# A three-block transformer layer on one core: attention's small work spread over other engines, and the last head's output tiles on two pairs of banks

## The reference

```python
x = x + 0.5 * ffn(layernorm(x), q_w, k_w, v_w, o_w, sel_v_w, sel_o_w, route_scale)
x = x + attention(layernorm(x), W_qkv, b_qkv, W_out, b_out)
x = x + 0.5 * ffn(layernorm(x), ...)                      # the same weights again
# x: (4, 512, 128) float32
# attention: 16 heads of 8 columns: softmax(q k^T / sqrt(8)) v, then W_out
# ffn: 8 heads of 128 columns, softmax attention in which value and output projection are
#      sums over 8 experts, gated by a top-2 of sigmoid(x @ sel) (normalised, times route_scale):
#   v   = sum_e gate_v[e] * (x @ v_w[h, e])
#   out = sum_h sum_e gate_o[h, e] * (softmax(q k^T / sqrt(128)) v) @ o_w[h, e]
```

## Time and profile before

| | us |
|---|---|
| median of 3 runs (1535.32 to 1540.82) | 1536.66 |
| the profiled execution | 1539.83 |
| its span, first to last instruction | 1538.0 |
| busy in the span: PE / DVE / ACT / POOL | 1477.0 / 1290.4 / 1205.5 / 978.5 |
| attention alone, from the last FFN slot to the first of the second FFN | about 690 to 881 |

### The profile page before, as it was taken

The page is one execution under the profiler, slowest core; times in us unless marked ns, Lnnn a source line. Parts: engine busy times, 40 slices in busy tenths (PEclk is TensorE's granted clock), DMA queues, the critical chain, the costliest instruction groups (busy, mean ns, idle before and its releaser), DMA issues.

```text
span 1538.0 us, 25896 instructions
## 1 busy us (share of the span) xinstructions
PE 1477.0 (96%) x7263; PEld 1104.9 (72%) x7263; DVE 1290.4 (84%) x3434; ACT 1205.5 (78%) x3587; POOL 978.5 (64%) x1719
## 2 busy tenths in 40 slices
PE   7899999999999999988998899999999999999997
PEld 5677888888888888743333358887888788888885
DVE  6899889888988877788878948988898889888885
ACT  3788888888888888748876778888888888888884
POOL 4578877776777677653240135777677767776665
PEclk9999999999999999999988999999999999999999
DMA  6244533322343225302211013333233333333321
GB/s 200 69 137 151 192 137 111 110 110 92 108 145 111 101 105 206 123 15 83 83 55 56 15 55 118 111 112 112 106 111 110 110 117 110 110 110 117 110 83 35
DMA packets 50837, 163.48 MB, mean 106 GB/s; under 512 B 3460, under 2 KB 26630, under 8 KB 34310
## 3 DMA queue, kind: packets, MB, share of 16 engines
q1 hardware_dynamic: 50694, 161.82, 30.0%
HBM read 136.64 MB, written 25.17 MB: 105 GB/s over the span
## 4 chain that ended last, share of the span: by engine, by line
PE 46%; DVE 7%; ACT 2%; issue 2%; POOL 1%; POOLq 0%; DVEq 0%; ACTq 0%
PE bank L523 10%; PE bank L524 10%; PE bank L525 10%; DVE mmax L1457 4%; PE bank L690 3%; PE bank L833 3%; PE bank L798 2%; PE bank L705 2%; PE bank L703 2%; PE bank L704 2%; DVE ot L1351 1%; ACT ot L1041 1%; PE bank L818 1%; PE bank L843 0%; ACT pm L1110 0%
## 5 line engine op out<-in xcount | busy, mean ns | idle before, releaser
L1002 ACT ACTIVATE vt<-bank,gate 128x128 f32<-128x128 f32 x1024 | 293.1, 374 | 105.2 <-PE bank L525 90.9
L1351 DVE SCALAR_TENSOR_TENSOR ot<-bank,gn,ot 128x128 f32<-128x128 f32 x1024 | 288.0, 344 | 70.0 <-ACT ot L1041 50.8
L1626 POOL TENSOR_TENSOR vt<-vt 128x256 f32<-128x256 f32 x256 | 197.8, 773 | 228.7 <-DVE vt L1337 227.9
L1041 ACT ACTIVATE ot<-bank,gn 128x128 f32<-128x128 f32 x1024 | 291.8, 372 | 24.9 <-PE bank L525 19.4
L1337 DVE SCALAR_TENSOR_TENSOR vt<-bank,gate,vt 128x128 f32<-128x128 f32 x1024 | 286.1, 342 | 11.5 <-ACT vt L1002 9.4
L1651 POOL TENSOR_TENSOR ot<-ot 128x256 f32<-128x256 f32 x256 | 197.5, 772 | 90.8 <-DVE ot L1351 86.9
L1360 DVE TENSOR_TENSOR pt<-bank,pt 128x512 fp32r<-128x512 f32 x256 | 175.6, 686 | 69.8 <-ACT pt L1029 69.4
L523 PE MATMUL bank<-wv,xhl 128*128 128x512 f32 x512 | 224.2, 438 | 3.0 <-DVE vt L1337 1.9
L523 PE MATMUL bank<-wo,chl 128*128 128x512 f32 x512 | 206.4, 403 | 7.9 <-DVE chl L1320 5.4
L1018 ACT ACTIVATE pp<-bank,nmin 128x512 f32<-128x512 f32 x256 | 178.1, 696 | 42.2 <-DVE nmin L1327 40.2
L1327 DVE TENSOR_REDUCE nmin<-bank 128x1 f32<-128x512 f32 x256 | 173.8, 679 | 37.0 <-PE bank L525 33.4
(11 more groups left out here) (192 smaller groups left out, 3000.7 us busy)
## 6 DMA issues: line engine op xcount, KB each, us to landing
wv<-wv_split SPq DMA_DIRECT2D x56, 1024.0 KB, 4.8
wo<-wo_split SPq DMA_DIRECT2D x56, 1024.0 KB, 4.8
wv_split<-wv SPq DMA_DIRECT2D x8, 1024.0 KB, 5.0
wo_split<-wo SPq DMA_DIRECT2D x8, 1024.0 KB, 7.1
qk<-qk_rows SPq DMA_DIRECT2D x32, 256.0 KB, 2.9
qk_rows<-qs SPq DMA_DIRECT2D x24, 256.0 KB, 2.9
rawv<-in_L_ffn_v_w SPq DMA_DIRECT2D x8, 512.0 KB, 6.2
rawo<-in_L_ffn_o_w SPq DMA_DIRECT2D x8, 512.0 KB, 8.2
```

The lines of the kernel that those rows point to most:

```text
L1002: last = activation(vt[:, u % 2, e * P:(e + 1) * P], gb[0][:, e * P:(e + 1) * P], ACT.Copy, scale=gate[:, n % 2, k, h * E + e:h * E + e + 1])
L1041: last = activation(ot[:, u % 2, e * D:(e + 1) * D], gb[2][:, e * D:(e + 1) * D], ACT.Copy, scale=gn[:, j % 2, k, e:e + 1])
L1351: last = v.scalar_tensor_tensor(o, gb[3][:, e * D:(e + 1) * D], gn[:, j % 2, k, G + e:G + e + 1], o, ALU.mult, ALU.add)
L1626: own.link(g_.tensor_tensor(a[:, 0:2 * P], a[:, 0:2 * P], a[:, 2 * P:4 * P], ALU.add))
```

## The change

1. **Last head** (its four tiles, in f = 1): the odd tiles' output products go to banks 0 and 1, which the value products have left, instead of 2 and 3, and PE waits for the reading of tile i - 2 rather than i - 1. DVE makes the first fold of 256 columns itself, right after its four instructions and before it releases the tile; POOL makes the two others.
2. **split_maxima** goes from DVE to POOL, in the same step.
3. **over_sums**: ACT copies the group's transposed outputs with their sums out of bank 5 to a new buffer oR (copy_sums, one instruction of 144 columns a group, in the step in which DVE did its part), and this releases the bank. Once a batch, at r = 37 (SUMS), DVE takes one reciprocal of 64 columns, and POOL one product of 512 columns. It was a reciprocal of 16 and a product of 128 columns on DVE in each group.
4. commit_x(B) goes from DVE to POOL (s = 173).
5. TURN_NEXT 29 to 26, TURN_AGAIN 172 to 170, LOGITS_AGAIN 178 to 176, RANK_AGAIN 190 to 198; the four reciprocals of 128 columns become eight of 64, at s = 181 to 195.

```diff
-AGAIN, TURN_AGAIN, LOGITS_AGAIN, RANK_AGAIN = 160, 172, 178, 190
+AGAIN, TURN_AGAIN, LOGITS_AGAIN, RANK_AGAIN = 160, 170, 176, 198
-PUT_VALUES, TURN_NEXT, TURN_OUTPUT, PUT_OUTPUT = 12, 29, MU + 13, MU + 17
+PUT_VALUES, TURN_NEXT, TURN_OUTPUT, PUT_OUTPUT = 12, 26, MU + 13, MU + 17
+SUMS = MU - GU + TURN_OUT + 2
+        def last_head(f, i):
+            return f == 1 and i >= TILES - QT
+        def output_bank(f, i, half):
+            return gb[half if last_head(f, i) and i % 2 == 1 else 2 + half]
# PE, released
-                    pe.wait_ge(on_ready, i + 1)
+                    pe.wait_ge(out_copied, i + 1)
# PE, outputs
-                    if u >= 1:
+                    if last_head(f, i) and i > TILES - QT:
+                        if i == TILES - QT + 1:
+                            pe.wait_ge((v_act, v_dve)[half], 2 * TILES)
+                        else:
+                            pe.wait_ge(free, u - 1)
+                    elif u >= 1:
                         pe.wait_ge(free, u)
# PE, output_transposes
-                    pe.wait_ge(on_ready, NG * (b + 1))
+                    pe.wait_ge(on_ready, b + 1)
# ACT
+                def copy_sums(G):
+                    b, g = G // NG, G % NG
+                    act.wait_ge(ott_mm, G + 1)
+                    if g == 0 and b >= 1:
+                        act.wait_ge(on_ready, b)
+                    o = place(("out", G))[:].rearrange("p (k j r) -> p k j r", k=QT, j=GH)
+                    activation(oR[:, :, GH * g:GH * g + GH, :], o[:, :, :, 0:DH + 1], ACT.Copy).then_inc(out_copied, 1)
# DVE, outputs
+                    if last_head(f, i):
+                        own.link(last)
+                        a = ot[:, u % 2, :]
+                        last = v.tensor_tensor(a[:, 0:2 * D], a[:, 0:2 * D], a[:, 2 * D:4 * D], ALU.add)
                     last.then_inc(o_dve, 1)
# DVE, mha: split_maxima and the per-group over_sums are gone; a batch's reciprocal remains
+                def over_sums(b):
+                    dve.wait_ge(out_copied, NG * (b + 1))
+                    if b >= 1:
+                        dve.wait_ge(on_ready, b)
+                    v.reciprocal(mrd[:], oR[:, :, :, DH]).then_inc(mrd_ready, 1)
-                    if s == TURN_AGAIN + 3:
-                        commit_x(B)
-                    if LOGITS_AGAIN + 4 < s < LOGITS_AGAIN + 13 and (s - LOGITS_AGAIN) % 2 == 1:
-                        k = (s - LOGITS_AGAIN - 5) // 2
+                    if LOGITS_AGAIN + 4 < s < LOGITS_AGAIN + 21 and (s - LOGITS_AGAIN) % 2 == 1:
+                        k, c = divmod((s - LOGITS_AGAIN - 5) // 2, 2)
                         own.settle()
-                        own.then(v.reciprocal(xn[:, k, :], xn[:, k, :]))
+                        own.then(v.reciprocal(xn[:, k, c * HE:(c + 1) * HE], xn[:, k, c * HE:(c + 1) * HE]))
# POOL, fold_outputs
-                    own.link(g_.tensor_tensor(a[:, 0:2 * D], a[:, 0:2 * D], a[:, 2 * D:4 * D], ALU.add))
+                    if not last_head(f, i):
+                        own.link(g_.tensor_tensor(a[:, 0:2 * D], a[:, 0:2 * D], a[:, 2 * D:4 * D], ALU.add))
# POOL, mha: split_maxima(G) as it stood on DVE, and
+                def over_sums(b):
+                    pool.wait_ge(mrd_ready, b + 1)
+                    if b >= 1:
+                        pool.wait_ge(ont_mm, b)
+                    g_.tensor_tensor(oN[:], oR[:, :, :, 0:DH], mrd[:].unsqueeze(3).to_broadcast([P, QT, NH, DH]), ALU.mult)\
+                        .then_inc(on_ready, 1)
# POOL, step: first of all in the step
+                    if batch_of(s - LAG, SUMS) is not None:
+                        over_sums(batch_of(s - LAG, SUMS))
+                    if group_of(s, GU - 1) is not None:
+                        split_maxima(group_of(s, GU - 1))
+                    if s == TURN_AGAIN + 3:
+                        commit_x(B)
```

More of the change, by code:

```diff
@@ L724, in outputs @@
                     e = slice(half * G, (half + 1) * G)
-                    split3(gb[2 + half][:], chl[:, j % 2, 0, c], chl[:, j % 2, 1, c],
+                    split3(output_bank(f, i, half)[:], chl[:, j % 2, 0, c], chl[:, j % 2, 1, c],
                            wo[:, j % 2, 0, e, :], wo[:, j % 2, 1, e, :]).then_inc(done, 1)
@@ L1040, in outputs @@
                     for e in range(G):
-                        last = activation(ot[:, u % 2, e * D:(e + 1) * D], gb[2][:, e * D:(e + 1) * D], ACT.Copy,
+                        last = activation(ot[:, u % 2, e * D:(e + 1) * D], output_bank(f, i, 0)[:, e * D:(e + 1) * D], ACT.Copy,
                                           scale=gn[:, j % 2, k, e:e + 1])
@@ L1133, in step @@
                         copy_out(group_of(i, TURN_OUT - 2))
+                    if group_of(i, TURN_OUT + 1) is not None:
+                        copy_sums(group_of(i, TURN_OUT + 1))
                     if batch_of(s, PUT_VALUES + 1) is not None:
@@ L1503, in step @@
                         row_max(s)
[L1504 to L1507, removed]
+                    if batch_of(i, SUMS) is not None:
+                        over_sums(batch_of(i, SUMS))
                     if batch_of(i, PUT_OUTPUT + 1) is not None:
@@ L1597, in input_rest, with commit_x @@
                     .then_inc(mx_lo, 1)
+            def commit_x(n):
+                pool.wait_ge(x_hi, n + 1)
+                g_.tensor_tensor(xhl[n % 2][:, 1, :], xT[:, n % 2, :], xhl[n % 2][:, 0, :].bitcast(F32), ALU.subtract)\
+                    .then_inc(prep_done, 1)
             def clear_attention():
@@ L1687, in mha, with split_maxima @@
             def mha():
+                def split_maxima(G):
+                    pool.wait_ge(m_max, GU * (G + 1))
+                    if G == 0:
+                        pool.wait_ge(mrow_set, 1)
+                    else:
+                        pool.wait_ge(m_tr, G)
+                    own.link(g_.tensor_copy(mrow[:, :, :, 3], mmax[:, G % 2, :, :]))
+                    g_.tensor_tensor(mrow[:, :, :, 7], mmax[:, G % 2, :, :], mrow[:, :, :, 3].bitcast(F32), ALU.subtract)\
+                        .then_inc(m_split, 1)
+                def over_sums(b):
[4 more added lines that the diff above has]
+                        .then_inc(on_ready, 1)
                 def add_maxima(G):
```

7 lines of the change are left out of this document (5 added, 2 removed).

## The result

| | before | after |
|---|---|---|
| median of 20 runs each, side by side | 1539.74 | 1532.11 |
| ratio (95% interval) | | 0.9953 (0.9944 to 0.9963) |
| profiled execution / its span | 1539.83 / 1538.0 | 1530.61 / 1528.8 |
| DVE busy / POOL busy | 1290.4 / 978.5 | 1277.4 / 988.5 |

The change makes the kernel 0.5% faster, 7.2 us by the ratio; 11.6 had been forecast. On another occasion the same kernel gave 0.9967 (0.9954 to 0.9980), 5.1 us (experiment 6). The median of 1536.7 that the forecast started from was that of three runs; twenty gave 1539.7. So 1532.1 lies in the range of 1516 to 1534, but the gain is smaller than forecast: of the 7.1 us between 1525 and 1532.1, 3.0 are the starting point and the rest is gain that did not come.

The account below looks back on a forecast made before the run. DVE was taken to bound attention, PE the two FFNs. 10.4 - 1.0 - 2.0 + 2.9 + 1.3 = 11.6 us faster, median 1536.7 to 1525; range 1516 to 1534 for 8 in 10.

Parts of the forecast that it names:

- DVE's relief, 10.4 us: Attention: work taken off DVE, plus the earlier input transposes, makes the stage 10.4 us faster; bounds 0 and 13.
- What takes over: Attention: ACT's added copies and small gaps lose 1 us, bounds 0 and 4; POOL's added work stays hidden.
- plain groups over 11 us: Attention: groups of 16 steps without stacks, forecast at 10.4 us, 10.8 with a residual; staying over 11 refutes the prediction.
- Rival (a): Attention: another engine is next, relief shows by half, 5 us instead of 10.4; about 6 gained, 1531; chance 0.24.
- TURN_NEXT, 1.2 us: Attention, three batches: earlier input transposes let the stack find xhl ready, ending PE's 0.43 us wait; 1.2 us gained.
- They cost nothing: Attention: POOL's two moved operations of 16 columns a group, 0.24 us each, needed by PE only 5 us later.
- The second FFN's input, 2 us lost: Step 170: over_sums delays POOL's xn, PE waits 3 us, outT then waits for bank 5; 2 us lost, bounds 0 and 3.
- The clock: Attention: half reciprocals keep PE busier, the second fall (820 to 834) goes or shrinks; 2.9 us gained, bounds 6 gained, 3 lost.
- The first fall: Clock fall at 792 to 804, while bank 5 changed hands: worth 3.2 us, stays or moves by some microseconds.
- 0.6 us more an operation: Attention: cost of moving elementwise work to POOL by the skill's rule, 1.28 against 0.62 us; counts only if POOL ends a wait.
- The last head, 1.3 us: Kernel's end: PE's second tile need not wait, DVE makes the first fold; 1.3 us gained, bounds 0.5 and 2.
- rival (d): Last head: ACT's tiles still come 2.2 us apart because of ot; 0.3 instead of 1.3 us; goes along with any case.

Follow-up runs that it names:

- experiment 6: Changed kernel repeated unedited, 0.9967 of the kernel before; four variants with the second FFN's input moved or unread products added, 0.9944 to 0.9986.
- Experiment 2: Attention's row maximum over 384 of 512 columns: 0.9941 in the kernel before, 0.9891 in the changed kernel, both against the kernel before.
- 3b: Attention's context over 256 of 512 queries: 1.0102 in the changed kernel, 1.0135 in the kernel before, both against the kernel before.
- experiment 4: Kernel before with split_maxima, over_sums and commit_x(B) off DVE alone, 1.0024; with TURN_NEXT 26 alone, 1.0002; with both, 0.9973.
- experiment 5: Kernel before with eight half reciprocals for four whole ones and the picks from step 198, alone: 0.9998 of the kernel before.
- moves_and_next: Kernel before with split_maxima, over_sums and commit_x(B) off DVE and TURN_NEXT 26, the rest unchanged: 0.9973 of the kernel before.

## Why the prediction was right or wrong

**DVE's relief, 10.4 us: wrong, the main miss.** Its failing sentence is the one in the first part: "Attention is bound by DVE"; with it the 1.0 us put down under "What takes over" was too small. The work did leave DVE (43.41 of 50 where more steps were done), but the seven groups from step 47 to 159 went from 86.4 to 83.6 us, and 1.8 of these 2.8 are the two groups with the transposes. By the forecast's own terms these seven should have won about 6 us (an estimate: 0.9 for each of six, half of it for the heavy one, 0.4 for each of the two with transposes, less 0.55 for the batch's reciprocal). The five without transposes won 0 to 0.3 us, not 0.9 each. The sign that the prediction gave for being wrong, plain groups over 11 us, came true at the edge: 11.0 to 11.6. Rival (a) was the case, and stronger than given (it let half of the relief show): not another engine alone, but the loop maximum, product, context, product through three banks, at 2.69 us for four steps where DVE's maxima need 2.48. Experiment 2 shows that DVE's work is not the bound in these seven groups, and that it is in the groups with the picks; 3b agrees for one group that it becomes so once the context is short. That PE and DVE alone close the loop is read from the timeline; ACT's part in it was left untested. The hint lay in the earlier trace rows: both DVE and PE wait for each other there, which is a loop and not slack of PE.

**TURN_NEXT, 1.2 us: the mechanism missed half.** The 0.43 us were read rightly from before (alone it gives 0.4 us in each of two groups); that split_maxima, once moved, stands ahead of input_rest on POOL in the same step was not seen. "They cost nothing" was wrong for who waits behind them. With TURN_NEXT as it was, the moves made the kernel 0.2% slower (experiment 4).

**The second FFN's input, 2 us lost: right place, too small.** PE's wait was 3.25 against 3 forecast. DVE had fewer maxima in hand than assumed and waited 3.78 at once; the wait cost 2.3 to 3.7 us, by which pair of runs one takes, and the clock 2.2 to 3.2, nearly 6 against a group without either.

**The clock: right in direction, not for the reason, and luck for the total.** The second fall went, and the groups to 191 and 207 won 4.7 us (2.9 forecast): more than all that the seven groups before them won. But half reciprocals alone only pushed it back (experiment 5). In after it doesn't come in the picks either; that DVE's relief keeps PE denser there is argued, not shown, and in moves_and_next, with the relief but whole reciprocals, falls stand at 817 to 825 and 855 to 862. The first fall was expected to stay; of four profiles of before and its small variants one has it whole (19.1), one in part (16.7) and two not at all (15.2), so it was in part chance of the one profile, and its cost should not have been taken from there. (The small idle times between groups of matmuls, which the prediction cites from the Trainium skill under HAM oscillation, stand on that page one section further, under "A second HAM failure mode: psum-queue depth-cycling".)

**ACT and POOL: the durations were right.** The copy took 0.32 us in the mean (0.27 to 0.4 forecast), the product on POOL 1.08 (1.28), the half reciprocal 0.54 (0.55), the fold on DVE 0.42. The "0.6 us more an operation", which the prediction took from the Trainium skill's rule and two rows of 512 columns, doesn't hold for 16 columns: there POOL took 0.21 and 0.23 us where DVE had taken 0.18 and 0.19.

**The last head, 1.3 us: right,** 1.45 in the timeline, and ACT waits for what was said; rival (d) is out. The times of the run can't show it.

**The starting point.** The profile and the three runs gave 1539.8 and 1536.7; twenty runs of before run from 1535.3 to 1546.1 but for one of 4958.8. The 3.2 us between the two, carried over as fixed, were chance.

Open: the 1.1 us between the last split and the second FFN's first head, which no run singles out; what ACT's part in the loop is worth; and whether the loop would give way all over with short contexts if the clock stayed up.

## What to carry to other kernels

Where two engines each wait for the other in small pieces through a few banks, write the round out in time (which instruction frees, which stands in between, which starts) before taking a busy share for a bound: relief of one engine is worth at most what the stage takes beyond that round. When work moves to an idle engine, read what stands behind it in the same step there. And take what a fall of the clock costs from several profiles.

## What the runs showed of the hardware

- Less work on PE can be slower: half the context's columns made the kernel after 1.5% and the kernel before 1.4% slower, and the granted clock was then 1.2 GHz in most of attention (0.51 in 704 to 726). With whole contexts that stretch is at 2.4 GHz.
- Twenty products that nobody reads, put into a wait of 3.25 us, kept the clock up there (1.00 instead of 0.57 in 798 to 810). The Trainium skill (TensorE: Matmul & The Clock Gate, What's actually happening) says that activity releases the throttle; these numbers agree. Waits of 0.93 and 0.86 us in the same steps had a fall behind them as well (0.57 in 802 to 810).
- Context products of four heads, each 16 columns wide and written to partitions of its own, took 1.05 us; those of two heads 1.04 us.
- Two profiles of the kernel after differ in their falls of the clock (675 to 679 in one alone; 798 to 809 in one, 802 to 810 in the other), and the groups at the full clock repeat to 0.1 us.
- GpSimd took 0.21 and 0.23 us for the two operations of 16 columns for which VectorE had taken 0.18 and 0.19, and 1.08 us for a product of 512 columns.
